# Top-k over two halves of every row, and attention and experts in one block without a barrier

## The reference, cut to what matters

```python
x = layernorm(x + attention(x))            # 8 sequences x 512 tokens x 256, 16 heads of 16, causal
scores = softmax(einsum('bsd,ed->bse', x, router_w))      # 8 experts
gate, idx = top_k(swapaxes(scores, 1, 2), 129)            # per sequence and expert: 129 of 512 tokens
tokens = x[b, idx]                                        # a gather of rows
h = gelu(tokens @ w1[e] + b1[e])                          # 256 -> 1024
y = (h @ w2[e] + b2[e]) * gate                            # 1024 -> 256
out = zeros.at[b, idx].add(y)
x = layernorm(x + out)
```

## Time and profile before

| | us |
|---|---|
| median of 3 runs | 938.88 (936.50 to 939.31) |
| profiled execution, its own time | 939.66 |
| its span | 937.7 |
| PE busy | 821.0 (88%) |
| DVE / ACT / POOL busy | 621.6 / 532.4 / 470.7 |
| granted TensorE clock, mean | 0.948 |

### The profile page before, as it was taken

The page is one execution under the profiler, slowest core; times in us unless marked ns, Lnnn a source line. Parts: engine busy times, 40 slices in busy tenths (PEclk is TensorE's granted clock), DMA queues, the critical chain, the costliest instruction groups (busy, mean ns, idle before and its releaser), DMA issues. The chain is left out here.

```text
span 937.7 us, 17098 instructions
## 1 busy us (share of the span) xinstructions
PE 821.0 (88%) x5864; PEld 614.0 (65%) x5864; DVE 621.6 (66%) x2033; ACT 532.4 (57%) x1042; POOL 470.7 (50%) x639
## 2 busy tenths in 40 slices
PE   4658999999999999988639599999999999999990
PEld 3434455454645454434229598999999999999990
DVE  4457778878787887999837893555545463646454
ACT  2126666767675867565617344556565655556555
POOL 6335665756656564333456507545344353535343
PEclk9878999999999999988869799999999999999996
DMA  4997687868686958620124314433525262523258
GB/s 139 168 154 148 102 148 142 154 102 162 106 165 117 148 110 146 140 70 2 45 79 153 79 51 61 92 76 57 125 46 136 35 148 35 141 30 48 34 134 259
DMA packets 90102, 100.52 MB, mean 107 GB/s; under 512 B 8736, under 2 KB 83488, under 8 KB 89888
## 3 DMA queue, kind: packets, MB, share of 16 engines
q1 hardware_dynamic: 72560, 77.92, 39.8%
q0 software_dynamic: 12800, 16.92, 11.2%
q10 hardware_dynamic: 4656, 4.59, 1.5%
HBM read 65.38 MB, written 33.62 MB: 106 GB/s over the span
## 5 line engine op out<-in xcount | busy, mean ns | idle before, releaser
L525 DVE CUSTOM_DVE_ANT_0 n_ps<-n_ps,tri 128x512 f32<-128x512 f32 (+3 forms) x512 | 238.7, 519 | 85.2 <-PE n_ps L655 83.7
L441 ACT ACTIVATE pt<-st_ps 128x512 f32<-128x512 f32 x320 | 184.3, 602 | 67.7 <-PE st_ps L640 52.5
L1190 PE MATMUL y_ps<-w_parts,h_hi 128*128 128x256 f32 (+1 forms) x1152 | 213.4, 280 | 0.9 <-DVE w_parts L1104 0.7
L1039 ACT ACTIVATE g<-h_ps,b 128x384 f32<-128x384 f32 (+1 forms) x192 | 103.9, 541 | 169.3 <-PE h_ps L1176 142.4
L1176 PE MATMUL h_ps<-tt_hi,w_parts 128*128 128x384 f32 (+1 forms) x768 | 171.0, 325 | 12.2 <-DVE w_parts L1104 10.3
L1011 POOL DMA_INDIRECT acc<-y,tok_no x64 | 102.8, 1606 | 153.5 <-DVE y L1128 147.1
L1190 PEld LDWEIGHTS y_ps<-w_parts,h_hi 128*128 128x128 f32 (+1 forms) x1152 | 172.4, 178 | 4.6 <-ACT h_hi L1044 1.5
L381 POOL TENSOR_SCALAR_AFFINE_SELECT pt<-pt 128x256 f32<-128x256 f32 (+1 forms) x320 | 110.1, 361 | 125.6 <-ACT pt L441 124.8
L1114 DVE TENSOR_TENSOR h_lo<-g,h_hi 128x384 fp32r<-128x384 f32 (+1 forms) x176 | 90.1, 513 | 121.1 <-ACT h_hi L1044 100.6
L1190 PE MATMUL y_ps<-w_parts,h_lo 128*128 128x256 f32 (+1 forms) x576 | 161.1, 280 | 0.0
L640 PE MATMUL st_ps<-w_parts 99*128 99x512 bf16 (+3 forms) x512 | 126.4, 309 | 17.9 <-ACT pt L441 15.4
(11 more groups left out here) (160 smaller groups left out, 1092.6 us busy)
## 6 DMA issues: line engine op xcount, KB each, us to landing
w_parts<-part_d SPq DMA_DIRECT2D x192, 128.0 KB, 6.3
w_raw<-in_w SPq DMA_DIRECT2D x16, 1024.0 KB, 5.5
part_d<-w_raw SPq DMA_DIRECT2D x96, 128.0 KB, 6.1
w_raw<-in_xt SPq DMA_DIRECT2D x8, 512.0 KB, 4.7
res<-in_x SPq DMA_DIRECT2D x8, 512.0 KB, 10.3
x<-res SPq DMA_DIRECT2D x8, 512.0 KB, 3.3
acc<-res SPq DMA_DIRECT2D x8, 512.0 KB, 5.0
fin<-acc SPq DMA_DIRECT2D x4, 512.0 KB, 3.9
```

What stands on the lines that cost most here:

```text
L441: nc.scalar.activation(pt[:, slot % PT_RING, n % UP, :], st_ps[at % ST_RING][:, :], ACT.Exp, scale=S_SCALE).then_inc(exp_done, 1)
L525: ins = nc.vector.tensor_tensor_reduce(out=src[:, h, :], in0=src[:, h, :], in1=mask, scale=-1.0, scalar=-BIG_NEG, op0=ALU.add, op1=ALU.min ...
L1039: nc.scalar.activation(g[:, at % G_RING, 0:cols], h_ps[at % H_RING][:, 0:cols], ACT.Gelu, bias=b1[:, e, n:n + 1]).then_inc(g_done, 1)
L1190: ins = nc.tensor.matmul(y_ps[at % Y_RING][0:rows, 0:C], x[:, q % 2, m, toks], w[e % 2][:, m, :], start=i == 0, stop=i == len(terms) - 1)
```

## The change

- **Two halves.** Each row of 512 scores becomes two rows of 256. `take_halves` (DVE, two copies) lays the scores out so that one transpose puts the first halves on partitions 0 to n-1 and the second halves on 64 to 64+n-1 (n = 48 early, 16 late). The 17 rounds run on [64+n, 256] instead of [n, 512] and give a sorted list of each half. The largest 129 of both lists, as a set, are found by comparing the first list with the second read backwards: the larger of each pair. `turn_halves` (eight transposes instead of two) and a matmul with a mirror matrix (`joined`) bring the two lists together; six small DVE instructions select, five more on one partition do the same for the 129th, which then goes by the two small DMAs.
- **Places.** Early: `halved` at place 33 and `pick` at 35 of sequence 6; two rounds at 37 and 39 of sequence 6, fifteen in sequence 7, none in the drain; `picked`, `joined` and `fetch` at place 3 of the drain, so ahead of both `cut` on POOL (w1's moves from place 1 to 4). Late: turning the rows moves from the head of the experts' stream to (-1, 3); rounds (2, 7, 8); `picked` (2, 3), `joined` (2, 4).
- **One block.** Both functions use one block; semaphores live through both. In place of the barrier the experts' streams wait for the last use of a PSUM bank by the attention (`dve_free`), for the scores, and POOL for the x1 stores only before the first gather of LEFT. PSUM tensors are allocated in another order.
- **Bias.** b1 is loaded with expert 0's weights during sequence 7; b2 stays at the head of the experts' SP stream.

```diff
-CUTS_AT = ((B, 1), (B, 12))
-ROUND_AT = [(B - 1, place) for place in (1, 2, 8, 11, 12, 16, 17, 23, 25, 26, 32, 38, 39)]
-ROUND_AT += [(B, place) for place in (1, 5, 12, 16)]
+CUTS_AT = ((B, 4), (B, 12))
+PICK_AT = ((B - 2, 33), (B - 2, 35), (B, 3))
+ROUND_AT = [(B - 2, place) for place in (37, 39)]
+ROUND_AT += [(B - 1, place) for place in (2, 8, 11, 12, 14, 16, 18, 20, 23, 25, 27, 29, 31, 34, 37)]
...
+def take_halves(nc, halves, scores, seqs):
+    n = (seqs.stop - seqs.start) * E
+    for half in range(2):
+        yield nc.vector.tensor_copy(halves[:, :, half * B_AT:half * B_AT + n],
+                                    scores[:, 2 * half:2 * half + 2, seqs, :].rearrange("p t b e -> p t (b e)"))
+def put_halves(nc, ps, halves, n, ident):
+    for t in range(2):
+        ins = nc.tensor.transpose(ps[0:B_AT + n, t * P:(t + 1) * P], halves[:, t, 0:B_AT + n], ident[:, :])
+    return ins
+def turn_halves(nc, ps, best_f, best, n, ident):
+    rows = B_AT + n
+    for row, first, last, at in ((P, 0, 1, 0), (1, P, 0, 4 * n + B_AT)):
+        for x, begin, col in ((best_f, first, 0), (best, first, n), (best, last, 3 * n), (best_f, last, 2 * n)):
+            ins = nc.tensor.transpose(ps[0:row, at + col:at + col + rows], x[:, begin:begin + row], ident[0:rows, 0:rows])
+    return ins
...
-    row_pool = [sb(f"row_pool{n}", [early, T], F32) for n in range(2)]
+    row_pool = [sb(f"row_pool{n}", [both_halves, HALF], F32) for n in range(2)]
...
-        sp.wait_ge(x1_out, 32 * B)
         sp.wait_ge(left_in, 32)
-        sp.wait_ge(ahead["w1_in"], 16)
-        sp.wait_ge(ahead["w2_in"], 16)
+        sp.wait_ge(dve_ready, dve_no[("proj", B - 1, TT - 1)] + 1)
...
-PICKED_AT = (2, 3)
-ROUNDS_IN = (5, 6, 6)
+PICKED_AT, JOINED_AT = (2, 3), (2, 4)
+ROWS_AT = (-1, 3)
+ROUNDS_IN = (2, 7, 8)
...
 (experts, DVE)
+        dve.wait_ge(seen["scored"], B)
+        for ins in take_halves(nc, halves, scores, slice(EARLY, B)):
+            ins.then_inc(halved, 1)
...
+            elif stage == "joined":
+                second = [pick_ps[:, at * late:(at + 1) * late] for at in range(2)]
+                dve.wait_ge(sides_in, 2)
+                a_no, a_by, b_no, b_by = (ends[:, at:at + late] for at in (0, late, 2 * late + B_AT, 3 * late + B_AT))
+                link(nc.vector.tensor_tensor(end_side[:, :], a_by, b_by, ALU.is_ge))
+                nc.vector.tensor_tensor(end_gate[:, :], a_by, b_by, ALU.max).then_inc(left_out, 1)
+                link(nc.vector.scalar_tensor_tensor(end_no[:, :], a_no, -float(HALF), b_no, ALU.add, ALU.subtract))
+                link(nc.vector.tensor_tensor(end_no[:, :], end_no[:, :], end_side[:, :], ALU.mult))
+                nc.vector.scalar_tensor_tensor(end_no[:, :], end_no[:, :], float(HALF), b_no, ALU.add, ALU.add).then_inc(left_out, 1)
+                dve.wait_ge(mirrored, 1)
+                ...
+                nc.vector.tensor_tensor(tok_no[:, EARLY:B, :], no[:, :].rearrange("p (b e) -> p b e", b=LATE), base_i[:, :, :], ALU.add).then_inc(picked, 1)
                 dve.wait_ge(left_in, 32)
+                dve.wait_ge(seen["left_in"], 32)
                 nc.vector.tensor_tensor(left_no[:, :], left_f[:, :], lbase_i[:, :], ALU.add).then_inc(picked, 1)
...
 (experts, PE)
+            elif stage == "joined":
+                pe.wait_ge(sides_in, 2)
+                nc.tensor.matmul(pick_ps[:, 0:2 * late], mirror[:, :], sides[:, 2 * late + B_AT:],
+                                 start=True, stop=True).then_inc(mirrored, 1)
```

More of the change, by code:

```diff
@@ L162, in weight_parts, with attention @@
     return both[:, 0, :, :], both[:, 1, :, :]
-def attention(nc, ctx, xt_d, x_d, wqkv_d, wp_d, wpn_d, rw_d, x1_d, acc_d, ident, scores, chosen, w1_d, w2_d, ahead):
+def attention(nc, block, both, ctx, xt_d, x_d, wqkv_d, wp_d, wpn_d, rw_d, x1_d, acc_d, ident, mirror, halves, scores, chosen, w1_d, w2_d, b1_d, ahead):
     def sb(name, shape, dt):
@@ L371, in _ @@
         link(nc.gpsimd.memset(zero[:, :], 0.0))
-        nc.gpsimd.iota(base_i[:, :], pattern=[[T, EARLY]], base=0, channel_multiplier=0).then_inc(bases, 1)
+        nc.gpsimd.iota(base_i[:, :], pattern=[[T, EARLY]], base=HALF, channel_multiplier=0).then_inc(bases, 1)
+        nc.gpsimd.memset(halves[:, :, :], 0.0).then_inc(bases, 1)
+        link(nc.gpsimd.memset(mirror[:, :], 0.0))
+        nc.gpsimd.affine_select(out=mirror[:, :], in_=mirror[:, :], compare_op=ALU.not_equal, fill=1.0, base=1 - P,
+                                pattern=[[1, P]], channel_multiplier=1).then_inc(bases, 1)
         for stage, b, n in steps():
@@ L601, in _ @@
             elif stage == "picked":
[L602 to L606, removed]
+                nc.vector.tensor_copy(sides[:, :], ps[:, 0:4 * early + B_AT]).then_inc(sides_in, 1)
@@ L815, in expert_steps @@
     yield "turn", 0, 0
-    yield "rows", 0, 0
     for q in range(-1, NQ):
@@ L859, with experts @@
 ADDS = adds_before()
-def experts(nc, ctx, x1_d, acc_d, w1_d, b1_d, w2_d, b2_d, out_d, ident, scores, chosen, ahead):
+def experts(nc, block, both, ctx, seen, x1_d, acc_d, w1_d, w2_d, b2_d, out_d, ident, mirror, halves, scores, chosen, ahead):
     def sb(name, shape, dt):
@@ L867, in sem @@
     def sem(name):
[L868 removed]
+        return both.enter_context(nc.semaphore(name))
     late = LATE * E
     tok_no, gate, left_f, left_gate = (chosen[n] for n in ("tok_no", "gate", "left_f", "left_gate"))
[L872 to L875 removed]
+    both_halves = B_AT + late
+    row_pool = [sb(f"late_pool{n}", [both_halves, HALF], F32) for n in range(2)]
+    best = sb("late_best", [both_halves, 8 * ROUNDS], F32)
+    best_at = sb("late_best_at", [both_halves, 8 * ROUNDS], U32)
+    best_f = sb("late_best_f", [both_halves, 8 * ROUNDS], F32)
+    sides = sb("late_sides", [P, 4 * late + B_AT], F32)
+    ends = sb("late_ends", [1, 4 * late + B_AT], F32)
+    first_side = sb("late_first_side", [P, late], F32)
+    no = sb("late_no", [P, late], F32)
+    end_gate = sb("late_end_gate", [1, late], F32)
+    end_side = sb("late_end_side", [1, late], F32)
+    end_no = sb("late_end_no", [1, late], F32)
     base_i = sb("late_base_i", [P, LATE, E], I32)
```

161 lines of the change are left out of this document (111 added, 50 removed).

## The result

The changed kernel takes **932.92 us** (median of 13 runs, 930.66 to 936.10), the kernel before 939.93 beside it (13 runs, 935.53 to 942.08): ratio **0.9932, 95% interval 0.9919 to 0.9946**. The forecast was 931.5. The profiled execution took 932.33 us on its own clock (before 939.66), its span is 930.6 (before 937.7).

The account below looks back on a forecast made before the run. PE bounds the back half (busy 326.3 of 327 us from 573), so earlier gains arrive whole. 4.5 + 4.4 + 4.3 - 4.7 - 0.5 = 8.0 us off 939.66 gives 931.7, set at 931.5 us; 8-in-10 range 923 to 938.

Parts of the forecast that it names:

- A round: Selection round on DVE: 2.29 us falls to 1.49 with 256 columns less, at 0.267 us saved per instruction.
- the slower rival: Selection instructions do not get shorter with fewer columns, rounds stay 2.29 us; about 948 us in all; chance 8%.
- Sequence 7: Attention's sequence 7, where DVE sets the pace: shorter rounds gain 4.5 us (2 to 6).
- Drain and barrier: From the last exp to up of job 0: no barrier and POOL's new order gain 4.4 us (2.5 to 6).
- The 7 us that the prediction puts behind rstd: Barrier's time between rstd and up of job 0: 7 us become 1.6.
- Opening: Experts' start, up of job 0 to up of job 2: w1's low parts come sooner, gain 4.3 us (2.6 to 7).
- PE needs 28.1 us as before: Experts' start: PE's time from up of job 0 to its arrival at up of job 2 stays 28.1 us.
- Late results: Turn of job 4: the longer chain to the LEFT gather loses 4.7 us (3 to 7), plus 0.5 for the clock.
- The fixed 2 us: Small DMAs of the late results: a fixed cost of some 2 us, making the loss an estimated 0.5 us more.
- The back half: From 573 to 900 us, bound by PE: the change touches nothing, so all earlier gain arrives whole at the end.
- if PE's stretch behind it isn't full: Sign that the prediction is wrong: PE not fully busy behind the turn of job 4.
- joining eats it: POOL's order, the low piece, the LEFT chain and sequence 7 leave 1.4 us of gain, about 938 us; chance 10%.

Follow-up runs that it names:

- rstd_first: The changed kernel with POOL's cuts of expert 0's second weight (9.8 us) moved from ahead of the last rstd to behind it; ratio 0.9888 (0.987 to 0.9905).

## Why the prediction was right, and where it was not

The time (931.5 for 932.9) is right within what can be measured, and most of what was to be seen came as told: rounds of 1.5 us, POOL's order, the wait of 6.4 us for w1's parts (the wait at the turn of job 4 was 4.6, forecast 5 to 7). But two of its steps failed, the opening by 1.7 us and the back half by 2.9. Errors of the other sign at three others covered them in the profiled pair: 1.35 in sequence 7 (most of it scatter between executions, see below), 1.2 in the drain, 1.8 at the late results. That the sum is so close is luck; the mechanisms ahead of 573 are not.

- *A round*: 1.49 forecast, 1.52 measured. The slope of another DVE instruction on the same engine carried over. The difference is the prediction's arithmetic: 716 and 333 ns at 512 and 128 columns make 255 ns for 256 columns, not 267, and so a round of 1.52. With it the slower rival fell, whose bound was 1.85.
- *Sequence 7, 4.5*: 5.85 in the profiled pair. The logits came at 445.6, forecast 447, and PE ran at 0.93 where it had run at 0.83. But E is not a constant: over ten executions with this same front part it lay at 455.9 to 459.4 (mean 457.5), over four with the old one at 461.9 to 462.6 (mean 462.3). By these means the term is 4.8. Most of this spread arises ahead of sequence 7: counted from its first exp, E is 51.5 to 52.0 us away in the four and 45.5 to 47.4 in the ten, means 51.7 and 46.5. That is 5.2 us for sequence 7, and sequence 6 with its two rounds is 0.2 longer, so it is even as forecast. Size right.
- *Drain and barrier, 4.4*: 5.57 in the pair. The chain ran as told, each link a little earlier (forecasts moved to the same E): POOL's gathers at E+2.8 (E+3.7), rstd at E+20.2 (E+21.1), up of job 0 at E+26.3 (E+27.4). POOL's new order gave back 0.64, not 1.6. The barrier alone is worth 6.15. The 7 us that the prediction puts behind rstd are 7.7 by its own rows (494.35 less 482.04 and 4.6), and these less the 1.6 for the tokens' parts are 6.1.
- *Opening, 4.3*: **2.6**. This term was mis-sized, and the step that failed is "PE needs 28.1 us as before". It needed 29.3: up of job 0 now begins behind 14.1 us of standing, and its first 13 matmuls, up to the turn of job 1, ran wholly at half the clock, 3.98 us for 2.80. The prediction had charged the clock behind the later stop only. So DVE's last run of work (from 506.72) began 23.8 us behind up of job 0 instead of 22.55, which is 1.2 of the missing 1.7 us. From there to up of job 2 it was 11.9 us for a forecast of 11.7, in which y was held by 1.8 (2.16 for 0.35) where 1.5 on a piece had been added. The last 0.2 is arithmetic: 532.69 less 528.6 is 4.1, not 4.3. The Trainium skill's "SBUF: two separate sides" in "SBUF — State Buffer" says that the loser of the shared ports blocks for a whole instruction. The trace agrees: y ended 0.16 us behind POOL's instructions, `ve` 0.04 behind its cuts, and the small `lg` of rstd_first came to 0.94 and 1.19 us. It also shows more than one instruction: `ve` was held through six of the cuts. By this rule the prediction gave 2.9 for the whole term. That 2.6 was measured is no proof of it: 1.2 us of the shortfall arose ahead of these instructions.
- *Late results, -4.7 and -0.5 for the clock*: -3.43, of which -3.9 behind S and 0.5 ahead of it. The turn came at S+19.5, forecast S+20.3; most of the difference is the way from POOL's first gather to the turn, 4.8 us for 5.4. From the start of SP's second issue to left_no it was 1.55 us, inside the bounds of 1.3 to 4.2; the prediction's terms make 1.7 of it. The fixed 2 us that the prediction gives from the Trainium skill's "DMA: Bandwidth & Descriptors" did not show here: 1.55 us is the measurement, and it is less. The half us for the clock was not due, since the old wait of 2.0 us had cost the same 1.4 already.
- *The back half: "the change touches nothing in it, and whatever is gained before 573 arrives whole at the end"*: **wrong by 2.9 us**. PE's matmuls and their order are the same there, but the places of their operands changed, by 832 bytes, and each matmul of the back half starts some 1.2 ns later behind the one before it. Shown by undoing it in the changed kernel and by doing it alone in the old one. The prediction read the diff for instructions and queues and did not look at what its new tensors push. Its sign of being wrong, "if PE's stretch behind it isn't full", could not tell: the stretch is full (313.37 of 314 us).

The rival "joining eats it" named two of the losses (the port, the LEFT chain), but they stayed near their forecast sizes. In the sum, 931.7 and 930.9 halve to 931.3, not 931.5, which changes nothing. A last 0.6 us lies behind the last turn. From there to the end it is 52.7 us in the kernel before and 53.2 and 54.4 in two executions of the changed one, with the last add and load of acc on the chain of waits each time; its cause stays open.

## What to carry to other kernels

Where one engine is bound by thousands of equal instructions, a new tensor anywhere below its operands is part of the change: compare the distance between the starts of two matmuls before and after, because the busy share (full in both) doesn't show it. Moving work to the far side of a dependence does not stop it from holding up the engine that runs beside it: of 4.9 us gained at rstd 3.1 were left. And a stop of PE costs its length and the stretch at the lower clock behind it. In the two sizes of wait seen here, 2.0 and 4.6 us, the second part was the same, and only the kernels whose wait had shrunk to 0.5 us or less got it back.

## What the runs showed of the hardware

- The start-to-start distance of fp32 matmuls (128 x 128 stationary, 256 columns moving) depends on where tensors lie in a partition: 116.4 ns with the weights and the token and h pieces at offsets 192 and 160 within 512 bytes, 117.8 at 192 and 480, 119.1 at 0 and 0. A shift of all tensors behind the identity by 1536 bytes changes nothing (116.4). In a `down` the stationary operand, h, is the one whose place changed; in an `up` it is the moving one, the tokens, and there the wide steps went from 173.7 to 174.7 ns too. What in the offset decides, and with what period, stays open; the offsets 160 and 480 differ by 64 within 128 as well.
- MAX8, FIND_INDEX8 and MATCH_REPLACE8 went from 682, 677 and 668 ns at 512 columns to 423, 419 and 409 at 256, on 112 partitions instead of 48: 1.01 ns a column and 0.15 to 0.16 us fixed. The number of partitions costs nothing: 16 take the 0.68, 0.67 and 0.66 us of 48, and 80 the 0.42, 0.41 and 0.40 of 112.
- A 0.17 us DVE instruction took 7.13 us beside eight back-to-back POOL instructions (466.91 to 476.72): it did not get in between them. In rstd_first, beside four such pieces, DVE did get in between them, one instruction at a time. What decides between the two stays open.
- Between identical instruction streams, on several chips, the end of the attention part, E, differs by up to 3.5 us from execution to execution (455.9 to 459.4), so that a term of 2 us can't be read from one pair of profiles unless it is counted from a milestone close by. From E to up of job 0 it was 26.29 to 26.30 us in five of these executions.
